# Attention in head groups on one core: the last head of a group and the K transposes of the next

## What is computed

```
q = (xn @ Wq.T) ; k = (xn @ Wk.T) ; v = (xn @ Wv.T)      # 32, 8 and 8 heads of 128
q = rmsnorm(q, q_norm_w) ; k = rmsnorm(k, k_norm_w)
scores = einsum("bkgqd,bksd->bkgqs", q, k) / sqrt(128)
attn = softmax(scores + where(rel > 0, -1e30, slope * rel))
s = einsum("bkgqs,bksd->bkgqd", attn, v) -> heads side by side @ Wo.T
x + s * silu(ffn(xn))
```

## Time and profile before

| | us |
|---|---|
| median of 3 runs | 1316.87 |
| lowest and highest | 1316.11 and 1317.1 |
| profiled execution | 1317.21 |
| its span in the trace | 1315.4 |
| mean granted clock of TensorE, share of full | 0.996 |
| busy: TensorE | 1282.7 |
| busy: VectorE | 972.9 |
| busy: GpSimd | 689.8 |
| busy: ScalarE | 651.6 |

### The profile page before, as it was taken

One profiled execution on the slowest core, in us unless ns is written; L12 is line 12 of the kernel. 1 busy time (PEld: TensorE's weight loads), 2 busy tenths in 40 slices (PEclk: granted clock), 3 DMA queues, 4 the chain that ended last, 5 costly groups with the idle time before them and its releaser, 6 DMA issues.

```text
span 1315.4 us, 20982 instructions
## 1 busy us (share of the span) xinstructions
PE 1282.7 (98%) x7135; PEld 1101.5 (84%) x7135; DVE 972.9 (74%) x2087; ACT 651.6 (50%) x1425; POOL 689.8 (52%) x746
## 2 busy tenths in 40 slices
PE   7899999999999999999999999999999999999997
PEld 6788888888888888888888888888888878888886
DVE  6777787778777877787778777877788864555556
ACT  4555555555555555555555555555565533222222
POOL 3555564555455545554555455545555625555553
PEclk9999999999999999999999999999999999999999
DMA  3000100000000000000000000000020036445441
GB/s 122 17 17 17 33 17 17 17 33 17 17 17 33 17 17 17 33 17 17 17 33 17 17 17 33 17 17 17 17 65 18 8 82 191 128 128 128 128 128 65
DMA packets 29469, 57.89 MB, mean 44 GB/s; under 512 B 3648, under 2 KB 3648, under 8 KB 29248
## 3 DMA queue, kind: packets, MB, share of 16 engines
q1 hardware_dynamic: 29376, 56.68, 15.1%
HBM read 54.57 MB, written 2.10 MB: 43 GB/s over the span
## 4 chain that ended last, share of the span: by engine, by line
PE 90%; DVE 6%; issue 1%; POOL 1%; ACT 1%; DMA 0%; DVEq 0%; SPq 0%; POOLq 0%
PE O L935 32%; PE O L1010 15%; PE S L1522 11%; PE T L956 10%; PE S L978 5%; PE S L976 5%; PE S L975 5%; DVE pb L729 2%; PE T L1029 2%; DVE pb L738 1%; PE O L1540 1%; PE T L1540 1%; PE O L1539 1%; PE T L1539 1%; PE O L1538 1%
## 5 line engine op out<-in xcount | busy, mean ns | idle before, releaser
L398 POOL TENSOR_TENSOR pb<-rel,coef 128x896 f32<-128x896 f32 (+1 forms) x255 | 292.0, 1159 | 127.7 <-PE T L956 120.4
L502 ACT ACTIVATE pb<-pb,low 128x1024 f32<-128x1024 f32 (+7 forms) x256 | 199.0, 777 | 190.4 <-DVE low L729 188.5
L492 ACT ACTIVATE pt_h<-T 128x512 fp32r<-128x512 f32 (+3 forms) x384 | 185.8, 487 | 117.1 <-PE T L956 114.0
L713 DVE TENSOR_TENSOR pt_l<-T,pt_h 128x512 fp32r<-128x512 f32 (+3 forms) x384 | 210.3, 550 | 42.4 <-ACT pt_h L492 42.4
L729 DVE CUSTOM_DVE_ANT_0 pb<-S,pb,ninv 128x1024 f32<-128x1024 f32 (+7 forms) x256 | 207.6, 811 | 40.4 <-PE S L978 35.3
L956 PE MATMUL T<-ident,pb 128*128 128x128 f32 x1152 | 190.2, 274 | 16.8 <-DVE pb L738 8.7
L956 PEld LDWEIGHTS T<-ident,pb 128*128 128x128 f32 x1152 | 141.1, 141 | 55.8 <-issue 15.3
L738 DVE TENSOR_SCALAR pb<-pb,rinv 128x1024 f32<-128x1024 f32 (+7 forms) x256 | 171.5, 670 | 9.0
L975 PE MATMUL S<-kT_h,q_h 128*128 128x512 f32 x382 | 141.1, 369 | 0.0
L1010 PE MATMUL O<-pt_h,v_h 128*128 128x512 f32 (+2 forms) x384 | 140.5, 366 | 0.0
L375 POOL TENSOR_TENSOR inv<-ms,cst 128x4 f32<-128x4 f32 x64 | 76.4, 1193 | 118.3 <-DVE ms L761 118.3
(11 more groups left out here) (171 smaller groups left out, 2882.8 us busy)
## 6 DMA issues: line engine op xcount, KB each, us to landing
wq_in<-in_wq SPq DMA_DIRECT2D x32, 256.0 KB, 2.8
wo_in<-in_wo SPq DMA_DIRECT2D x32, 256.0 KB, 2.6
stage<-in_wkv SPq DMA_DIRECT2D x8, 512.0 KB, 3.9
stage<-in_gate_w SPq DMA_DIRECT2D x14, 256.0 KB, 2.7
stage<-in_gate_z SPq DMA_DIRECT2D x14, 256.0 KB, 3.8
stage<-in_gate_s SPq DMA_DIRECT2D x14, 256.0 KB, 5.2
stage<-in_up_w SPq DMA_DIRECT2D x14, 256.0 KB, 5.3
stage<-in_up_z SPq DMA_DIRECT2D x14, 256.0 KB, 6.4
```

The lines of the kernel that those rows point to most:

```text
L398: g_.tensor_tensor(pbuf(idx, t), rel[:, TOK - w:TOK], coef[:, t:t + 1].to_broadcast([P, w]), ALU.mult).then_inc(bias_ready, 1)
L492: a_.activation(pt_lot(pt_h, t, n), bank[:, 0:m * P].rearrange("p (k w) -> p k w", w=P), ACT.Copy).then_inc(tr_hi, 1)
L502: a_.activation(pbuf(idx, t), pbuf(idx, t), ACT.Exp, bias=low[:, idx:idx + 1], scale=-1.0, accum_out=rsum[:, idx:idx + 1]).then_inc(exps_r ...
L713: v_.tensor_tensor(pt_lot(pt_l, t, n), bank[:, 0:m * P].rearrange("p (k w) -> p k w", w=P), f(pt_lot(pt_h, t, n)), ALU.subtract).then_inc( ...
```

## The change

In the last head of the steady groups (`swap`) the quarter of K and V (`kv_proj`, with its copy and squares) takes the place of the first half of the next head's Q projection, and that comes where the quarter of K and V was. In the last head of all groups but the last (`early_k`) TensorE does scores 7 ahead of the last PV half. The squares of Q go behind the sixth product of that half, and the K transposes of the next group behind its 20th; ScalarE and VectorE make kT_h and kT_l there too, ahead of the split of the PV output. The parts "ss1" (the squares) and (3, 0) exchange their T banks in these heads. The first head of a group then has the order of the others, with scores 0 first, and waits for kT_l there. GpSimd does `k_norm` for tiles 4 to 7 ahead of bias 7. The diff, its core:

```diff
@@ place_in_head
+    if h % PER == PER - 1 and h != HEADS - 1 and key in ("ss1", (3, 0)):
+        return PARTS.index((3, 0)) if key == "ss1" else PARTS.index("ss1")
@@ group_order
-            out += [f"qc1_{nx}"] * more + [f"w2_{j}"] * w + [f"kv{j}"] * (not last)
+            q, k = [f"qc1_{nx}"] * more, [f"kv{j}"] * (not last)
+            out += (k + [f"w2_{j}"] * w + q) if j == PER - 1 else (q + [f"w2_{j}"] * w + k)
@@ gpsimd, group
-                bias(h, 7)
                 if j == PER - 1 and not last:
                     k_norm(g + 1, 1)
+                bias(h, 7)
@@ scalar, group
-            if kind != "first":
-                act.wait_ge(kt_ready, g + 2)
-                kT_hi_part(g, slice(0, TOK))
...
-                if j > 0:
+                if prev:
                     exp(h, 0)
-                elif kind == "steady":
+                if j == 0 and kind == "steady":
                     wkv_hi_part(g + 1)
...
+                swap = kind == "steady" and j == PER - 1
+                if more and not swap:
                     q_hi(at, f"qc1_{(j + 1) % PER}")
                 lot(h, 4, 0)
                 exp(h, 4)
+                if swap:
+                    k_squares(at, [f"kv{j}"], g + 1)
                 lot(h, 4, 1)
                 exp(h, 5)
-                if kind == "first":
+                if swap:
+                    q_hi(at, f"qc1_{(j + 1) % PER}")
+                elif kind == "first":
...
                 lots(h, 2)
...
+                if kind != "last" and j == PER - 1:
+                    act.wait_ge(kt_ready, g + 3)
+                    kT_hi_part(g + 1, slice(0, TOK))
                 v_hi(at, f"v1_{j}", j)
@@ vector, group
-            if kind != "first":
-                normalise(g * PER - 1, 7)
-                dve.wait_ge(kt_hi, g + 2)
-                kT_lo_part(slice(0, TOK))
...
-                if more:
+                if swap:
+                    kv_copy(at, [f"kv{j}"], g + 1)
+                elif more:
                     q_lo(at, f"qc1_{nx}")
...
+                elif swap:
+                    q_lo(at, f"qc1_{nx}")
                 elif not last:
                     kv_copy(at, [f"kv{j}"], g + 1)
-                if more:
+                if j == PER - 1 and not last:
+                    k_mean_sq(g + 1, 1)
+                elif more:
                     mean_sq(h + 1, 1, part_no(h, "ss1"), T[place_in_head(h, "ss1") % 2])
                 logits(h, 6)
+                lots(h, 3)
                 if j == PER - 1 and not last:
-                    k_mean_sq(g + 1, 1)
-                lots(h, 3)
+                    logits(h, 7)
+                    mean_sq(h + 1, 1, part_no(h, "ss1"), T[place_in_head(h, "ss1") % 2])
...
                 lots(h, 2)
+                if j == PER - 1 and not last:
+                    dve.wait_ge(kt_hi, g + 3)
+                    kT_lo_part(slice(0, TOK))
                 v_lo(at, f"v1_{j}", j)
@@ tensor, group
-            else:
-                pe.wait_ge(kn_ready, NC * (g + 1))
-                pe.wait_ge(logits_ready, g * (PER * QT) - 1)
-                k_transposes(range(QT))
...
-                if j > 0:
+                if prev:
+                    if j == 0:
+                        pe.wait_ge(kt_lo, g + 2)
                     scores(h, 0)
...
+                swap, early_k = kind == "steady" and j == PER - 1, not last and j == PER - 1
+                if swap:
+                    kv_proj(at, f"kv{j}", g + 1, {3 * KT: [lambda h=h: lot(h, 5, 1)]})
+                elif more:
                     q_proj(at, f"qc1_{nx}", h + 1, {6: [lambda h=h: lot(h, 5, 1)]})
...
+                if swap:
+                    q_proj(at, f"qc1_{nx}", h + 1)
+                elif early_k:
+                    pass
...
+                if early_k:
+
+                    def next_k(g=g, h=h):
+                        pe.wait_ge(kn_ready, NC * (g + 2))
+                        pe.wait_ge(logits_ready, h * QT + 7)
+                        k_transposes(range(QT))
+
+                    scores(h, 7)
+                    values(at, f"v1_{j}", h, None, {6: [squares1], 12: [lambda h=h: lots(h, 2)], 20: [next_k]})
+                    w_unit(3)
```

More of the change, by code:

```diff
@@ L587, in group @@
                     lots(h - 1, 0)
-                if j > 0:
+                if prev:
                     exp(h, 0)
-                elif kind == "steady":
+                if j == 0 and kind == "steady":
                     wkv_hi_part(g + 1)
-                if kind == "first" and j == 0:
+                if not prev:
                     act.wait_ge(kt_ready, 2)
@@ L595, in group @@
                 q_hi(at, f"qc0_{j}")
-                if j == 0:
+                if not prev:
                     exp(h, 0)
@@ L822, in group @@
                 unit = 4 * (j % 2)
-                if prev and j > 0:
+                swap = kind == "steady" and j == PER - 1
+                if prev:
                     normalise(h - 1, 7)
-                if j > 0:
                     logits(h, 0)
-                if prev:
                     lots(h - 1, 1)
                     lots(h - 1, 0)
-                if j > 0:
                     normalise(h, 0)
@@ L833, in group @@
                     q_lo(at, f"qc0_{j}")
-                elif kind == "first":
+                else:
                     dve.wait_ge(kt_hi, 2)
@@ L899, in group @@
                     project(at, f"w3_{j}", unit + 3, kind == "first")
-                logits(h, 7)
+                if not (j == PER - 1 and not last):
+                    logits(h, 7)
                 if last and j == 1:
@@ L1180, in group @@
                 now = FIRST_KV[j][j == 0:2 - j] if kind == "first" else [f"kv{j}"] * (not last)
-                if now:
+                if swap:
+                    q_proj(at, f"qc1_{nx}", h + 1)
+                elif early_k:
+                    pass
+                elif now:
                     kv_proj(at, now[0], g + 1, {3 * KT: [squares1]})
@@ L1188, in group @@
                     kv_proj(at, "kv3", 1)
-                values(at, f"v1_{j}", h, g + 1 if j == 0 else None, {12: [lambda h=h: lots(h, 2)]})
-                w_unit(3)
-                scores(h, 7)
+                if early_k:
[6 more added lines that the diff above has]
+                    w_unit(3)
+                else:
+                    values(at, f"v1_{j}", h, g + 1 if j == 0 else None, {12: [lambda h=h: lots(h, 2)]})
+                    w_unit(3)
+                    scores(h, 7)
         group(0, "first")
```

## The result

| | us |
|---|---|
| before, median of 14 runs | 1315.85 (1314.94 to 1317.1) |
| changed, median of 14 runs | 1319.86 (1318.71 to 1321.49) |
| ratio | 1.0029, 95% interval 1.0021 to 1.0036 |
| profiled execution changed, its span | 1319.01, 1317.2 |

The change makes the kernel slower, by 4.0 us at the medians. The forecast was 1320.0 us, 3.1 us over the median that was known then; with more runs that median came out 1 us lower.

A forecast was written before the change was run, and what follows sets the result against it. TensorE, busy 98% of the span, was taken as the bound. Six steady boundaries at 0.36 us (2.2 us) plus the first made 3.1 us over 1316.87, hence 1320.0 us; range 1317.2 to 1322.8.

The forecast's parts named there:

- The old stall: TensorE's wait at lots 7 of a group's first head for VectorE's normalisation; removing it gains 7 x 0.60 = 4.2 us.
- The chain of 3.56 us against a cover of 2.73 us: First K transpose to kT_l against TensorE's work before scores 0: a wait of 0.83 us at each of seven boundaries.
- Restart 0.1 us, lots 2 0.1 us: Loss per boundary restarting at the first score product; wait at lots 2 for tile 3's T bank, in six groups.
- K norm is covered: GpSimd's k_norm in the last head is done at 288.69, ahead of the K transposes at 289.93; no wait.
- ScalarE's split of the K/V weights is hidden: One more ScalarE instruction behind exp 0 in a group's first head, costed at nothing; otherwise a few tenths.
- The sum of a steady boundary: Net loss at each later boundary: 0.83 + 0.10 + 0.10 - 0.60, 0.4 us; 0.36 us by absolute times, six times 2.2 us.
- The first boundary: Behind head 3: TensorE waits a microsecond at lots 2; loss 0.95 us in all (0.4 to 1.4).
- my own signs of being wrong: Scores starting without a wait, lots 7 of heads 4 and 8 under 130.4 us apart, or bias or logits as releasers.
- the case of smaller terms: Rival at the boundaries: wait 0.6 to 0.7 us, none at lots 2, half the first boundary; 1318.0 us, chance 0.27.
- that of a hidden chain: Rival at the boundaries: K chain fully hidden, no new wait replaces the old; 1313.7 us, chance 0.08.
- C: Rival in the last head: a late bias or held bank adds 0.3 us per boundary; 1322.1 us, chance 0.15.
- D: Clock rival: boundary waits each halve TensorE's clock, costing some 1.5 us at seven boundaries; 1333.6 us, chance 0.03.

The follow-up runs named there:

- The four places of the transposes: Changed kernel with K transposes behind product 24, 20 (the change), 16 or 13 of the last PV half: 1323.72, 1319.86, 1315.31, 1313.67 us.
- the halved chain: Changed kernel, transposes still behind the 20th product, but signalled after four and eight tiles, kT_h and kT_l made in two halves: 1315.45 us, ratio 0.9996.
- the kernels without the exchange: KV and Q projection put back in the last head: in the changed kernel 1318.81 us; with lots 2 and transposes behind the 13th product 1312.92 us.
- the best kernel: Changed kernel with lots 2 and K transposes behind the 13th product, head 3's scores 7 behind the 6th: 1312.38 us, ratio 0.9974.

## Why the prediction was right

- **The old stall is worth 0.60 us a boundary and goes.** Right. Lots 7 of head 8 follow scores 0 after 8.19 us (8.10 and a restart of 0.1 were said), and with every new wait removed the groups stand 129.85 us apart, 0.57 us less than before.
- **The chain of 3.56 us against a cover of 2.73 us.** Measured 3.57 and 2.74 us. All three durations and the hand-over came from rows of other places, and they held. The four places of the transposes and the halved chain show that this difference is the cause, not only a companion.
- **Restart 0.1 us, lots 2 0.1 us.** Measured 0.11 and 0.10 us. The reason for the second is as told: the T bank that VectorE holds with lots 3. It goes when lots 2 are moved by one product or when logits 6 come earlier.
- **K norm is covered.** Right; the changed kernel has it at 287.10, 2.0 us ahead of the transposes, and the kernels without the exchange waited for it neither behind the 20th nor behind the 13th product.
- **ScalarE's split of the K/V weights is hidden.** It shows in no wait of TensorE from 130 to 990 us.
- **The sum of a steady boundary was too small.** 0.36 us were said and 0.48 us measured. I had two sums, 0.43 us by terms and 0.36 us by absolute times, and took the lower without a reason. What the absolute times lacked was at lots 2: they start 0.15 us after VectorE's end, not 0.05 us, and from there to the K transposes it is 1.83 us, not 1.79 us. It counts six times: 0.7 us.
- **The first boundary: right size, wrong place.** 0.95 us were said and 1.0 us measured. But I had put the wait at lots 2 of head 3. It stands at scores 7. They write S[1], which logits 5 must have read, and logits 5 end at 152.47 where TensorE was ready at about 151.6. In the steady heads a projection stands between, and I had checked S[1] there only. Logits as a releaser was one of my own signs of being wrong, and here it came, once. The size held because VectorE sets when lots 2 can start, wherever TensorE does its waiting: they were expected 8.1 us behind lots 4 (150.29 to 158.4) and come 8.08 us behind (148.25 to 156.33). Moving scores 7 into the PV half won only 0.2 us, which fits; an order of VectorE made for this head was not tried.
- **The sign.** Slower by more than 0.2% had 0.53 and came; the case of smaller terms (0.27) and that of a hidden chain (0.08) did not. Nor did C (0.15): a steady boundary cost 0.12 us more than said and not 0.3 us, and from 160 to 990 us no bias and no logits are among the releasers. The clock stayed at 1.00 through all boundaries, so D is out: two waits of 0.7 us, 9 us apart, didn't lower it. Its time was added up wrongly besides: 1316.87 + 3.1 + 7 x 1.5 is 1330.5 us, and 1333.6 us has the 3.1 us twice. The chances don't depend on it.

That the forecast of 1320.0 us fell within 0.2 us of the median is partly luck. The change was under-priced by 0.9 us, and the median of before had been over-read by 1.0 us, from three runs.

## What to carry to other kernels

When a producer chain is moved under cover, add up the chain from trace durations (every engine and every hand-over) and the cover from the distance of starts, and place it by the difference; here the place was four to seven products too late, 0.8 us. With the transposes seven products earlier the kernel is 0.2% faster than before, and as changed it is 0.3% slower. If the place can't move, start the second engine on the first half. And when instructions change order, look for each double-buffered bank at what frees it in every variant of the loop, the first one too.

## What the start of the kernel showed

The runs of one kernel lie 2 to 3 us apart, and the traces show one likely reason. In the first group TensorE stands idle for 2.2 us ahead of head 0's lots 7, before and after the change. After it the clock fell to its lower level of 1.2 GHz in the profiled execution before, as the earlier trace rows showed, and not in that of the changed kernel, where TensorE does the same up to there. Two stretches of each, us, busy time and count of the engines, then PEclk. The kernel before:

```profile
42.00:46.00 4.00, 1.75 (x12) 1.23 (x11) 3.28 (x8) 2.16 (x5) 2.49 (x2) 0.95 0.01 2
46.00:50.00 4.00, 3.41 (x14) 2.89 (x13) 2.26 (x5) 2.02 (x4) 1.90 (x2) 0.62 0.02 4
```

The changed kernel:

```profile
42.00:46.00 4.00, 1.74 (x13) 1.33 (x12) 3.89 (x9) 2.10 (x5) 1.74 (x2) 1.00 0.01 2
46.00:50.00 4.00, 2.60 (x18) 1.98 (x16) 3.07 (x7) 3.39 (x8) 3.10 (x3) 1.00 0.17 52
```

So one idle time of 2.2 us may or may not cost half the clock for some microseconds, in the same code. Over an execution it shows in the mean clock: of the ten runs of the best kernel, the five with 0.997 took 1311.0 to 1311.8 us, the five with 0.994 to 0.996 took 1313.0 to 1314.0 us. Lots 4 of head 3 stand at 150.29 us in the trace before and at 148.25 us after, 2 us apart before the change has done anything: 0.75 us of it lie ahead of lots 7 of head 0 (45.10 and 44.35 us) and 1.29 us behind. The two spans (1315.4 and 1317.2 us) show only 1.8 us of the 4 us. That is why the distances within the steady groups were the better ruler here. The Trainium skill (TensorE: Matmul & The Clock Gate, Part 1) says that the number of slow matmuls at a kernel's start varies from run to run. Here it is a stretch 45 us in that varies, at a clock of 1.00 from 42 to 50 us in one trace and 0.62 from 46 to 50 us in the other. It isn't the only one: from 18 to 22 us the clock was 0.57 before and 0.63 in the changed kernel, but 1.00 in the trace of the best one, which in its turn shows 0.70 from 42 to 46 us. The forecast took no account of it.
